# Routed expert slots in units of 64 rows

## The reference

```python
xn  = layernorm(x)                                  # x: 8 x 512 x 256, 4096 tokens in all
att = softmax((xn @ k.T) * scale) @ v               # 1024 keys for each of 8 batches
shared = gelu(xn @ Wfc_s + bfc_s) @ Wproj_s + bproj_s     # 256 -> 1024 -> 256
p, i = top_k(softmax(xn @ Wr), 2); p = p / p.sum()        # 8 experts, two for a token
routed = sum over e of gate[:, e] * (gelu(xn @ Wfc[e] + bfc[e]) @ Wproj[e] + bproj[e])
out = x + att + shared + routed
```

## Time and profile before

| | |
|---|---|
| median of 3 runs | 770.95 us (770.71 to 771.51) |
| span of the profiled execution | 769.0 us |
| instructions | 21389 |
| PE busy | 756.3 us, 98% of the span |
| PE weight loads busy | 645.5 us, 84% |
| VectorE busy | 470.6 us, 61% |
| ScalarE busy | 449.6 us, 58% |
| GpSimd busy | 231.6 us, 30% |
| PE's share of the chain that ended last | 92% |
| DMA, mean over the span | 171 GB/s |

### The profile page before, as it was taken

The page is one execution under the profiler, slowest core; times in us unless marked ns, Lnnn a source line. Parts: engine busy times, 40 slices in busy tenths (PEclk is TensorE's granted clock), DMA queues, the critical chain, the costliest instruction groups (busy, mean ns, idle before and its releaser), DMA issues.

```text
span 769.0 us, 21389 instructions
## 1 busy us (share of the span) xinstructions
PE 756.3 (98%) x6963; PEld 645.5 (84%) x6963; DVE 470.6 (61%) x1161; ACT 449.6 (58%) x863; POOL 231.6 (30%) x272
## 2 busy tenths in 40 slices
PE   7999999999999999999999999999999999999998
PEld 6899866777777778999899988888888888888887
DVE  5887858888887797454544544444344444336776
ACT  6666546666668775556556565455544455544452
POOL 2445426656566752012122121121211221220000
PEclk9999999999999999999999999999999999999999
DMA  9657222657575958655523558546465646304565
GB/s 307 213 184 168 86 83 85 228 185 254 186 235 179 354 202 291 171 165 135 160 69 69 172 147 226 172 132 204 123 192 152 177 138 198 97 29 151 159 205 152
DMA packets 109949, 131.29 MB, mean 171 GB/s; under 512 B 64496, under 2 KB 91472, under 8 KB 103488
## 3 DMA queue, kind: packets, MB, share of 16 engines
q1 hardware_dynamic: 84784, 108.30, 46.4%
q0 software_dynamic: 6480, 17.77, 6.3%
q10 hardware_dynamic: 18624, 4.46, 2.9%
HBM read 89.32 MB, written 41.18 MB: 170 GB/s over the span
## 4 chain that ended last, share of the span: by engine, by line
PE 92%; DVE 3%; issue 2%; ACT 1%; DMA 1%; POOL 1%; ACTq 0%; DVEq 0%; POOLq 0%
PE ps_v L1413 32%; PE ps_h L1393 31%; PE ps_v L1573 11%; PE ps_h L1509 11%; PE ps_t L1523 4%; DMA slots_x<-x_split,pos_i 1%; PE ps_t L1344 1%; DVE h_split L1021 1%; PE ps_v L1471 0%; ACT h L804 0%; PE ps_v L1420 0%; PE ps_v L1344 0%; POOL slots_x L712 0%; PE ps_h L1445 0%; DVE v_split L1077 0%
## 5 line engine op out<-in xcount | busy, mean ns | idle before, releaser
L1021 DVE TENSOR_TENSOR h_split<-h,h_split 128x512 f16<-128x512 f32 (+1 forms) x224 | 142.3, 642 | 157.8 <-ACT h_split L810 157.6
L804 ACT ACTIVATE h<-ps_h,b_fc 128x256 f32<-128x256 f32 (+1 forms) x320 | 126.0, 444 | 156.2 <-PE ps_h L1393 156.2
L1393 PE MATMUL ps_h<-x_t,w_split 128*128 128x256 f16 (+1 forms) x1920 | 193.3, 261 | 0.1
L1413 PE MATMUL ps_v<-w_stage,h_split 128*128 128x256 f16 x1704 | 192.6, 273 | 0.2 <-DVE h_split L1021 0.2
L1393 PEld LDWEIGHTS ps_h<-x_t,w_split 128*128 128x128 f16 x1920 | 170.4, 98 | 17.4 <-issue 0.4
L1413 PEld LDWEIGHTS ps_v<-w_stage,h_split 128*128 128x128 f16 x1704 | 166.3, 98 | 19.5 <-issue 0.4
L748 POOL DMA_INDIRECT tokens_y<-prob,to_i x71 | 73.5, 1035 | 325.5 <-DMA tokens_y<-prob,to_i 177.6
L810 ACT CAST h_split<-h 128x512 f16<-128x512 f32 (+1 forms) x224 | 130.7, 584 | 10.0
L1509 PE MATMUL ps_h<-k_t,x_t 128*128 128x512 f16 x384 | 88.1, 379 | 1.7 <-issue 1.7
L1573 PE MATMUL ps_v<-v_split,p_t 128*128 128x256 f16 x768 | 88.9, 272 | 0.0
L804 ACT ACTIVATE h<-ps_h,b_t 128x256 f32<-128x256 f32 x128 | 53.5, 468 | 57.2 <-PE ps_h L1393 55.3
(11 more groups left out here) (162 smaller groups left out, 613.6 us busy)
## 6 DMA issues: line engine op xcount, KB each, us to landing
w_split<-wpack SPq DMA_DIRECT2D x17, 1024.0 KB, 5.7
w_stage<-wpack SPq DMA_DIRECT2D x17, 1024.0 KB, 5.3
wpack<-w_split SPq DMA_DIRECT2D x8, 1024.0 KB, 5.0
wpack<-h_split SPq DMA_DIRECT2D x8, 1024.0 KB, 5.0
y_rows<-tokens_y SPq DMA_DIRECT2D x32, 256.0 KB, 3.4
b_pj<-bias_e SPq DMA_DIRECT2D x40, 128.5 KB, 3.7
w_stage<-in_L_ffn_Wfc_dram SPq DMA_DIRECT2D x4, 1024.0 KB, 7.1
scale_b<-key_scale SPq DMA_DIRECT2D x8, 512.0 KB, 6.2
```

What stands on the lines that cost most here:

```text
L804: ins = nc.scalar.activation(h32[:, hc, 0:n], ps_h[:, hc * TILE:hc * TILE + n], ACT.Gelu_apprx_tanh, bias=bias[:, hc:hc + 1], scale=1.0 / WS)
L1021: ve.tensor_tensor(h_split[par][:, 1, 2 * b:2 * b + 2, 0:n], h32[:, 2 * b:2 * b + 2, 0:n], h_split[par][:, 0, 2 * b:2 * b + 2, 0:n], ALU.s ...
L1393: ins = mm(ps_h[:, hc * TILE:hc * TILE + cols], wv[:, wl, c, hc * P:(hc + 1) * P], x[:, xl * DC + c, 0:cols], start=n == 0, stop=n == 3 * ...
L1413: ins = mm(ps_y[a][:, :], h_split[par][:, xl, c, a * P:(a + 1) * P], wv[:, wl, c, :], start=n == 0, stop=n == 3 * HC - 1)
```

## The change

The unit becomes 64 rows. An expert's count is rounded up to 64; it gets fulls of 256, halves of 128 and quarters of 64. There are FULLS = 28, HALVES = 8 and QUARTERS = 7, 43 steps in place of 40. Even j are full; odd j are half below Q0 = 16 and quarter from 17 to 29; from MIXED = 30 on all are full. The last expert's count is rounded up to 256 for its fulls. A quarter's up product has 64 moving columns; its down product is that of a half, 24 matmuls of 256 columns, and its scatter writes 64 rows. The tables have three kinds in place of two; VectorE's chain on s_table grows (TABLE from 32 to 50). SyncE writes one block of zeros more; GpSimd fills two index rows more at the start (CONSTS from 17 to 19). The number of steps is odd now, so the last one has parity 0. The lengths of the loops on all engines follow.

```diff
-BLOCKS = (TOKENS * TOP + EXPERTS * (P - 1)) // P
-FULLS = (BLOCKS - EXPERTS) // 2
-HALVES = BLOCKS - 2 * FULLS
-ROUTED = FULLS + HALVES
-MIXED = 2 * HALVES
+UNITS = (TOKENS * TOP + EXPERTS * (UNIT - 1)) // UNIT
+HALVES, QUARTERS = EXPERTS, EXPERTS - 1
+FULLS = (UNITS - 2 * HALVES - QUARTERS) // 4
+SMALL = HALVES + QUARTERS
+ROUTED = FULLS + SMALL
+Q0, MIXED = 2 * HALVES, 2 * SMALL
...
-def is_half(j):
-    return j < MIXED and j % 2 == 1
+def size_of(j):
+    if j % 2 == 0 or j >= MIXED:
+        return TILE
+    return P if j < Q0 else UNIT
...
-            def load_slots(j, par, half, first=False):
+            def load_slots(j, par, n, first=False):
...
+                    sp.dma_start(rows(slots_x, first_pad + P, P), zeros[:, :, :]).then_inc(s_pad, 16)
...
-            with pairs(sp, 3, MIXED - 3) as j:
-                body2(j, 1, slots=(True,), this=True)
-                body2(j + 1, 0, slots=(False,))
-            for j in range(MIXED - 3, MIXED + 2):
-                body2(j, j % 2, slots=(is_half(j + 2),), this=is_half(j))
+            with pairs(sp, 3, Q0 - 1) as j:
+                body2(j, 1, slots=P, this=P)
+                body2(j + 1, 0, slots=TILE)
+            body2(Q0 - 1, 1, slots=UNIT, this=P)
+            body2(Q0, 0, slots=TILE)
+            with pairs(sp, Q0 + 1, MIXED - 1) as j:
+                body2(j, 1, slots=UNIT, this=UNIT)
+                body2(j + 1, 0, slots=TILE)
+            body2(MIXED - 1, 1, slots=TILE, this=UNIT)
+            body2(MIXED, 0, slots=TILE)
...
                 if u == 24:
                     settle()
-                    link(ve.tensor_tensor_scan(full_end, one_row[:, :], pair[:, :], 0.0, ALU.mult, ALU.add), wait=True)
+                    link(ve.tensor_tensor_scan(full_end, one_row[:, :], quad[:, :], 0.0, ALU.mult, ALU.add), wait=True)
                     link(ve.tensor_scalar(full_end, full_end, float(FULLS), None, ALU.min), wait=True)
-                    link(ve.tensor_tensor(full[:, :], full_end, ends[:, 0, 0:EXPERTS], ALU.subtract))
+                    link(ve.tensor_tensor(full[:, :], full_end, ends[:, 0, 0:EXPERTS], ALU.subtract), wait=True)
+                    link(ve.scalar_tensor_tensor(out=left[:, :], in0=full[:, :], scalar=-4.0, in1=unit[:, :],
+                                                 op0=ALU.mult, op1=ALU.add), wait=True)
...
-                    link(ve.scalar_tensor_tensor(out=odd[:, :], in0=full[:, :], scalar=-2.0, in1=blk[:, :],
+                    link(ve.tensor_scalar(left_i[:, :], left_i[:, :], 1, None, ALU.arith_shift_right), wait=True)
+                    link(ve.tensor_copy(twos[:, :], left_i[:, :]), wait=True)
+                    link(ve.tensor_tensor_scan(half_end, one_row[:, :], twos[:, :], 0.0, ALU.mult, ALU.add), wait=True)
+                    link(ve.tensor_scalar(half_end, half_end, float(HALVES), None, ALU.min), wait=True)
+                    link(ve.tensor_tensor(half[:, :], half_end, ends[:, 1, 0:EXPERTS], ALU.subtract))
...
-                if half:
+                if n == TILE:
+                    down(R0 + j, par, w_pj[par])
+                else:
                     down(R0 + j, par, w_pj[par], subs=(0,), each=SUB)
...
-            with pairs(pe, 1, MIXED - 1) as j:
-                body2(j, 1, this=True)
-                body2(j + 1, 0, prev=True)
+            with pairs(pe, 1, Q0 + 1) as j:
+                body2(j, 1, this=P)
+                body2(j + 1, 0, prev=P)
+            with pairs(pe, Q0 + 1, MIXED + 1) as j:
+                body2(j, 1, this=UNIT)
+                body2(j + 1, 0, prev=UNIT)
```

More of the change, by code:

```diff
@@ L595, in _, with body2 @@
             load_pj(0, 0, first=True)
-            load_tail(0, 0, False, first=True)
-            load_slots(2, 0, is_half(2))
-            def body2(j, par, slots=None, this=False):
+            load_tail(0, 0, TILE, first=True)
+            load_slots(2, 0, TILE)
+            def body2(j, par, slots=None, this=TILE):
                 if j is not LAST:
@@ L868, in step2 @@
                 act.wait_ge(s_bfc_in[par], nth(j, par))
-                gelu(R0 + j, par, b_fc[par], n=P if half else TILE)
+                gelu(R0 + j, par, b_fc[par], n=n)
             exp(0)
@@ L1182, in tables @@
                                                  op0=ALU.mult, op1=ALU.add))
-                    link(ve.scalar_tensor_tensor(out=half_from[:, :], in0=full[:, :], scalar=float(TILE), in1=region[:, :],
-                                                 op0=ALU.mult, op1=ALU.add), wait=True)
-                    link(ve.tensor_tensor_scan(half_end, one_row[:, :], odd[:, :], 0.0, ALU.mult, ALU.add))
                 if u == 26:
                     settle()
-                    for kind, lo, hi in kinds:
+                    link(ve.scalar_tensor_tensor(out=single[:, :], in0=half[:, :], scalar=-2.0, in1=left[:, :],
+                                                 op0=ALU.mult, op1=ALU.add))
@@ L1189, in tables @@
+                    link(ve.scalar_tensor_tensor(out=single_from[:, :], in0=half[:, :], scalar=float(P), in1=half_from[:, :],
+                                                 op0=ALU.mult, op1=ALU.add), wait=True)
+                    link(ve.tensor_scalar(single[:, :], single[:, :], 0.0, None, ALU.max), wait=True)
+                    link(ve.tensor_tensor_scan(single_end, one_row[:, :], single[:, :], 0.0, ALU.mult, ALU.add), wait=True)
+                    for kind, lo, hi, _each in KINDS:
                         each = [1, hi - lo, EXPERTS]
@@ L1269, in rows_of @@
                     dve.wait_ge(s_y_out, scattered(j - 1, 1 - par, mixed))
-                ve.scalar_tensor_tensor(out=to_i[par][:, 0:subs], in0=tail[par][:, 0:subs, 0], scalar=b_pj[par][:, D:D + 1],
-                                        in1=tail[par][:, 0:subs, 1], op0=ALU.not_equal, op1=ALU.add).then_inc(s_to, 1)
-            def evict2(j, par, half=False):
-                evict(R0 + j, par, b_pj[par], 1 if half else SUB, first=isinstance(j, int) and j < 2)
-            def body2(j, par, prev=False, this=False, following=False, mixed=True):
-                n = P if this else TILE
-                split_h(R0 + j, par, n, banks=(0, 1, 2))
+                ve.scalar_tensor_tensor(out=to_i[par][0:p, 0:n // p], in0=tail[par][0:p, 0:n // p, 0],
+                                        scalar=b_pj[par][0:p, D:D + 1], in1=tail[par][0:p, 0:n // p, 1],
+                                        op0=ALU.not_equal, op1=ALU.add).then_inc(s_to, 1)
@@ L1280, in body2, with evict2 @@
+            def evict2(j, par, n=TILE):
+                evict(R0 + j, par, b_pj[par], SUB if n == TILE else 1, first=isinstance(j, int) and j < 2)
+            def body2(j, par, prev=TILE, this=TILE, following=TILE, mixed=True):
+                split_h(R0 + j, par, this, banks=(0, 1, 2))
                 rows_of(j - 1, 1 - par, prev, mixed)
-                turn_slots(j + 1, 1 - par, n=P if following else TILE)
-                split_h(R0 + j, par, n, banks=(3,))
+                turn_slots(j + 1, 1 - par, n=following)
+                split_h(R0 + j, par, this, banks=(3,))
```

236 lines of the change are left out of this document (130 added, 106 removed).

## The result

The changed kernel takes 779.78 us (median of 4, 778.27 to 782.0) against 770.92 (4 runs): 1.0119 of the time before, 95% interval 1.0103 to 1.0135. It is 8.86 us slower. The forecast was slower by 3.95, 774.9, with a range up to 777.7: the sign held, the size did not. The profiled execution is the slowest of the four, 782.0 with a span of 780.2, so its trace holds some 2 us more than the median.

A forecast was written before the change was run, and what follows sets the result against it. TensorE bounds the mixed stretch, with SyncE a second engine at its limit. From a span of 769.0, the stretch's +1.05 (8.60 saved, SyncE's stalls against it) and the tables' +2.9 gave 772.95, 774.9 us as a time; range 769.5 to 777.7.

The forecast's parts named there:

- TensorE's columns: Mixed routed stretch: three full steps fewer, small steps costing 22.84 us more, so TensorE's work falls by 8.60 us.
- TensorE stalled by SyncE, steps 17 to 31: Full and quarter pairs: TensorE needs 14.50 us, SyncE 15.48, so TensorE stands still 7.2 to 12.2 us.
- tables: Routing tables on VectorE, tiles 23 to 27: 18 more operations, 3.04 us, of which 2.9 (1.8 to 3.2) reach TensorE.
- The rival of a fixed price by the weight load: Quarters' up products: each matmul costs its weight load's 87 ns, 4.20 us a product; 784.9 us, slower; chance 0.03.
- The mechanism: Steps 17 to 30: SyncE, without waits, becomes the bound; TensorE idles for late weights, 7 to 12 us in all.
- The first rival: Quarter stretch: TensorE stays the bound, SyncE's lag hidden by its lead of 7.06 us; 765.2 us, faster; chance 0.17.
- the nine loads: Weight loads on SyncE's queue within the seven pairs: 0.58 to 1.03 us each, 5.22 to 9.27 in all.
- SyncE's sum: SyncE's queue from step 17: pairs, loads and a deduction put step 31's b_fc issue at 545.15 to 549.65.
- the price of a pair without loads: SyncE's own work for two steps without weight loads: 15.48 us, times seven pairs 108.36.
- The deduction for the written-out steps: Three SyncE steps written out beside the loops go quicker, 6.98 us against 7.74: 3 x 0.76 = 2.28 deducted.
- the weights' way: The w_fc of step 31 was to land 4.9 to 5.4 us after its issue.
- The second rival: SyncE bounds as forecast, but the tables' delay is swallowed: 772.0 us (769.5 to 774.5), mostly no change; chance 0.15.

The follow-up runs named there:

- both heavier kernels: The kernel before with one, then two reads of tab_e more in each of SyncE's steps 3 to 14: 776.99 and 783.36 us.
- the filler: The changed kernel with 40 matmuls of 128 columns, whose result nobody reads, ahead of up2(0) at tile 30: 779.11 us.
- the kernel with the value product first: The changed kernel with the value product of query tile 29 put ahead of the first half of up2(0) on TensorE at tile 30: 775.99 us.

## Why the prediction was right in its sign and wrong in its size

The terms of the sum against what the runs gave for each, in us:

| term | predicted | measured |
|---|---|---|
| TensorE's columns | -8.60 | 14.50 a pair, 1.40 a quarter's up product, as predicted |
| TensorE stalled by SyncE, steps 17 to 31 | +9.7 (7.2 to 12.2) | +13.7 by difference (8.86 + 8.60 - 3.8); +13.99 in the trace (562.15 - 446.66 - 101.50) |
| tables | +2.9 (1.8 to 3.2) | +3.8 won back in the changed kernel, +2.8 alone |
| sum | +3.95 | +8.86 |

**The columns: right.** The line through the prices of 256 and 128 columns gave 29 ns for 64, and 1.40 / 48 is 29. The rival of a fixed price by the weight load falls: its 87 ns would have made the product 4.20. The Trainium skill, "TensorE: Matmul & The Clock Gate", section "Back-to-back issue gap", gives about 81 ns per matmul for a stream of weight loads and matmuls of 128 columns, by which the product would have taken an estimated 3.89 us. The trace disagrees with it: 1.40 us at 64 columns, and 55.8 ns per matmul at 128.

**The mechanism: right.** SyncE became the bound in the quarter stretch, without a wait, and TensorE stalled for weights; its 9.93 us of idle time lie in the 7 to 12 that were announced. The kernel with fewer reads shows that it was SyncE's own time, the one without reloads that the stalls were the weights' lateness. The first rival, with SyncE's lag hidden by its lead, falls with the result and with both heavier kernels. Half of it was right: without the nine loads the lead hid 6.6 us of lag.

**SyncE's sum: mis-sized.** This is the step that failed. I put the fourteen steps at 111.3 to 115.35, they took 117.14. The term at fault is above all the price of a pair without loads. The sum took 15.48, gave it no bounds, and multiplied it by seven. The pair ahead of it in the same trace, also without loads, had taken 402.86 - 387.18 = 15.68:

```profile
387.18 0.33 SPq L526 DMA_DIRECT2D b_fc<-bfct_d  x1
```

In the changed kernel the pair without loads shown above took 15.98, which alone makes 7 x 0.50 = 3.5 us. With it the range is 114.8 to 118.85, and 117.14 lies in it. The kernel without reloads tells the same another way: less its wait, its fourteen steps took 109.0, where the sum without loads has 108.36 - 2.28 = 106.08. The nine loads are then left with some 8.1, 0.90 each, inside the 0.58 to 1.03. The deduction for the written-out steps held: one of them with a weight load took 557.22 - 549.43 = 7.79, which is 6.98 and a load of 0.81. But the marks of steps 17 and 31 enclose two such steps and not three, so 0.76 too much was deducted. These parts come from different executions and add up roughly only. A smaller part is the weights' way, 5.74 us for step 31 where the sum had 4.9 to 5.4.

Where the 0.50 of the pair comes from is seen for the most part. Its twelve table reads took 3.50 us there and 3.23 in the pair of the earlier trace rows, and the tail of a 64-row step took 0.53 to issue, that of a 128-row step before 0.35:

```profile
539.21 0.53 SPq L565 DMA_DIRECT2D tail<-slots_x  x1
```

```profile
416.13 0.35 SPq L555 DMA_DIRECT2D tail<-slots_x  x1
```

A read isn't a constant (tab_e's reads in the changed kernel: count, shortest, median and longest in ns):

```profile
L514 SPq TENSOR_LOAD <-tab_e x168: 262/268/760, 292.9 to 678.2; - x168
```

**The tables: right alone, low in place.** 3.04 us of VectorE's work were predicted, tab_x came 3.30 later in the changed kernel, and in the kernel before the delay cost 2.8. In the changed kernel 3.8 could be won back. There up2(0) came 4.18 later: SyncE issued the first slots 3.19 later, and they took 1.1 us longer from issue to transpose (302.61 - 295.96 against 298.32 - 292.77); first the changed kernel, then the one before:

```profile
295.96 4.77 SPq L558 DMA_DIRECT2D x_split<-slots_x  x8
...
302.61 1.25 DVE L1268 STREAM_TRANSPOSE x_t<-x_split 128x1024 f16<-128x1024 f16 x1 [1.33 <-DMA x_split<-slots_x]
```

```profile
292.77 4.83 SPq L548 DMA_DIRECT2D x_split<-slots_x  x8
```

Why they did isn't settled. The prediction's 18 operations, moreover, have the four memsets of tile 22 among them, which it set apart: its 3.04 counts 0.32 too much. The second rival, that the delay is swallowed, falls.

**What the text left out:** that TensorE can come out of a stall with a lower clock. In the profiled execution of the changed kernel that made three stretches longer by 1.68, 1.67 and 1.52 us. The last two lie inside the stretch that SyncE paces. SyncE's queue waited for nothing there and TensorE still stood 1.48 us for w_fc of step 31 at its end, so in this execution they were time in which TensorE would have waited anyhow. At up2(0) the filler didn't show a gain that can be told from the spread, so it isn't a term of its own in the table.

## What to carry to other kernels

An engine that only issues DMAs appears in no busy share of the page; before the steps of a kernel are made more and smaller, its time for a step is to be measured in its own queue and set against the bounding engine's new time, for it is paid by step and not by column. A price that is multiplied by seven needs bounds of its own, from every row that shows it. An issuing queue that waits for nothing over a whole stretch goes at its own pace there, and its lead covers a load, as I read these runs, only by what is left after the transfer's own way. Where it becomes the bound, reads of the same table entry done once and the order of its issues decide whether the columns saved are seen at all: here they turned 8.9 us of loss into 7.1 of gain, with the tables' delay covered beside them.

## What the runs showed of the hardware that I had not expected

A read of one table entry into SyncE's register, with its range check, takes about 0.55 us (1.66 us for three, above), more than one DMA issue of 0.34 to 0.36, and it is not constant: the load itself takes 262 to 760 ns.

TensorE's granted clock was lower behind some stalls and full behind others of like length. The up2(0) of the changed kernel, and a quarter's up product behind a stall of 3.12 us in the kernel with the value product first (the granted clock is the third number from the end):

```profile
303.91:308.20 4.29, 4.29 (x24) 3.22 (x25) 2.27 (x5) 1.74 (x3) 0.00 (x0) 0.60 1.04 331
```

```profile
475.25 2.74 PE L1443 MATMUL ps_h<-x_t,w_split 128*128 128x64 f16 x48 [3.12 <-DMA w_split<-wpack]
```

```profile
475.25:478.00 2.75, 2.75 (x49) 2.69 (x50) 0.41 (x2) 1.68 (x8) 0.90 (x1) 0.50 0.12 17
```

The 0.50 is the level of 1.2 GHz for the whole product, 2.74 us in place of 1.56; the 0.60 is that level for most of it. In the changed kernel the matmuls were slow after stalls of 2.31, 2.78 and 3.03 us, and of usual length after 1.44, 1.48 and 1.67. But after 2.86 us in the kernel with fewer reads up2(0) took its usual 2.79, after 2.84 in the one with the filler an up product its usual 5.41, and after 2.94 in the one with the value product first a down product its usual 5.41.
